# Local attention fed from an input transposed once per tile, with inverse norms formed as exp(-0.5 ln)

## What is computed

```
for i in range(DEPTH):                                   # DEPTH = 6
    x = attn_layer(shift_tokens(x), Wqkv[i], q_scale[i], k_scale[i], Wo[i]) + x
    x = ffn_layer(shift_tokens(x), ...) + x

def shift_tokens(t):                # upper half of the features comes from the token before
    a, s = jnp.split(t, 2, -1)
    s = jnp.pad(s, ((0, 0), (1, 0), (0, 0)))[:, :-1]
    return jnp.concatenate([a, s], -1)

def attn_layer(x, Wqkv, qs, ksc, Wo):                    # 16 heads of 64
    q, k, v = split heads of x @ Wqkv
    q = l2norm(q) * qs;  k = l2norm(k) * ksc             # t / max(|t|, 1e-12)
    q = q * cos * scale + rotate_half(q) * sin * scale   # k with 1 / scale
    # blocks of 32 queries see their own and the preceding 32 keys, within a band
    sim = q . k * 8, masked;  out = softmax(sim) . v
    return out @ Wo
```

## Time and profile before

| | us |
|---|---|
| span of the profiled execution | 8256.2 |
| unprofiled runs, median of 3 | 8264.78 |
| lowest, highest | 8245.68, 8279.47 |
| PE busy | 6903.7 (84%) |
| DVE busy | 5790.4 (70%) |
| ACT busy | 3976.8 (48%) |
| POOL busy | 2842.2 (34%) |

### The profile page before, as it was taken

How to read it: one execution, slowest core, us unless ns; L and a number is a source line. 1 busy time by engine, 2 the same in 40 slices (tenths; PEclk the granted TensorE clock), 3 DMA queues, 4 the chain that set the end, 5 groups by cost and what they waited for, 6 DMA issues and landing times. The chain is left out here.

```text
span 8256.2 us, 273787 instructions
## 1 busy us (share of the span) xinstructions
PE 6903.7 (84%) x119720; PEld 4913.8 (60%) x119720; DVE 5790.4 (70%) x10595; ACT 3976.8 (48%) x6628; POOL 2842.2 (34%) x2110
## 2 busy tenths in 40 slices
PE   7999699999996998998998998998997779445566
PEld 3444478888885665665665665665665556345434
DVE  6666389999996885885885885885886557752366
ACT  3555145555553774775775775775775212210121
POOL 0101033323332773773773773773772000001000
PEclk8999599999998999999999999999998889555556
DMA  0000000000001221221221221221220000000000
GB/s 15 1 1 1 3 6 4 4 4 4 4 3 33 69 69 45 69 69 41 71 72 41 69 72 42 69 69 45 69 72 24 2 15 1 3 3 4 5 0 13
DMA packets 187955, 249.19 MB, mean 30 GB/s; under 512 B 58997, under 2 KB 85492, under 8 KB 185844
## 3 DMA queue, kind: packets, MB, share of 16 engines
q1 hardware_dynamic: 186740, 231.40, 10.6%
HBM read 27.84 MB, written 2.10 MB: 4 GB/s over the span
## 5 line engine op out<-in xcount | busy, mean ns | idle before, releaser
L1701 POOL TENSOR_TENSOR XNT<-XNT 128x1024 f32<-128x1024 f32 x384 | 908.8, 2367 | 309.0 <-DVE XNT L1875 309.0
L1775 PE MATMUL wa_front<-w_wqkv,wa_xsT 128*128 128x512 f32 x1920 | 951.6, 619 | 49.9 <-ACT wa_kT L1756 29.6
L1704 POOL TENSOR_TENSOR XNT<-XNT,wa_rnorm 128x1024 f32<-128x1024 f32 x320 | 608.8, 1902 | 349.1 <-DVE wa_rnorm L1883 349.1
L1872 DVE TENSOR_TENSOR XNT<-wa_front,w_scaled 128x1024 f32<-128x1024 f32 x320 | 381.7, 1193 | 292.8 <-ACT wa_sq L1721 292.8
L1775 PEld LDWEIGHTS wa_front<-w_wqkv,wa_xsT 128*128 128x128 f32 x1920 | 333.4, 193 | 314.0 <-issue 281.8
L446 PE MATMUL a0h_ring<-a0h_QT,a0h_KT 32*128 32x512 f32 (+3 forms) x1536 | 448.7, 556 | 14.3 <-ACT a0h_E L564 10.4
L564 ACT ACTIVATE a0h_E<-a0h_ring 128x512 f32<-128x512 f32 (+1 forms) x640 | 320.6, 555 | 287.6 <-PE a0h_ring L446 285.8
L1721 ACT ACTIVATE wa_sq<-wa_front 128x1024 f32<-128x1024 f32 x320 | 324.9, 1015 | 185.5 <-PE wa_front L1775 184.9
L1875 DVE TENSOR_TENSOR XNT<-wa_front,w_scaled 128x512 f32<-128x512 f32 x640 | 408.6, 680 | 0.0
L1887 DVE TENSOR_REDUCE wa_norm<-wa_sq 128x16 f32<-128x1024 f32 x320 | 386.8, 1209 | 0.0
L1781 PEld LDWEIGHTS wa_front<-consts,XNT 128*128 128x128 f32 x2560 | 292.7, 143 | 141.8 <-POOL XNT L1704 66.8
(11 more groups left out here) (632 smaller groups left out, 18051.1 us busy)
## 6 DMA issues: line engine op xcount, KB each, us to landing
wa_v_look<-wa_v_all SPq DMA_DIRECT2D x960, 128.0 KB, 2.4
wa_v_look<-wa_v_all SPq DMA_DIRECT2D x640, 64.0 KB, 2.0
wal_v_look<-wal_v_all SPq DMA_DIRECT2D x192, 128.0 KB, 2.3
wal_v_look<-wal_v_all SPq DMA_DIRECT2D x128, 64.0 KB, 2.0
w_wqkv<-in_L_ffn_Wqkv_dram SPq DMA_DIRECT2D x6, 1024.0 KB, 6.0
w_wo<-in_L_ffn_Wo_dram SPq DMA_DIRECT2D x6, 512.0 KB, 6.7
w_wqkv<-in_L_ffn_Wqkv_dram SPq DMA_DIRECT2D x12, 256.0 KB, 7.1
f2w_raw<-in_L_ffn_w_dram SPq DMA_DIRECT2D x48, 64.0 KB, 1.9
```

The source lines that it names most:

```text
L1701: g.tensor_tensor(rot[:, at], rot[:, at], part[:, at], ALU.add).then_inc(s[summed], 1)
L1704: g.tensor_tensor(rot[:, at], rot[:, at], spread(rnorm[:, at, :], HDW), ALU.mult).then_inc(s[done], 1)
L1775: last = pe.matmul(front[:, first + i, :], xsT[:, slot, :], wqkv[:, (2 * n + i) * 512:(2 * n + i + 1) * 512], start=True, stop=True)
L1872: v.tensor_tensor(rot[:, n], src, cos, ALU.mult)
```

## The change

The shifted input is no longer made by three products. A new stage of the pipeline, `fetch`, runs one step ahead of `turn_in` (so there is a 36th step, k = -1). PE transposes the tile once, straight out of `Y`, into the first bank of the Q product's PSUM pair, and ACT copies the two halves to `xT`, the upper half one column further right. `xT` holds the eight tiles of a sequence side by side, for two sequences, and its column 0 is zero; `x_of` gives the 128 columns of a tile. `y`, `xsT` and the POOL copy are gone.

The DVE operation on `norm` is now a `tensor_scalar` with one tensor input instead of a `tensor_tensor` with two, and the DVE reciprocals of the norms are gone.

The order on the engines changes too. The K product is squared by ACT at the start of the next step instead of at the end of its own, and the rotation of K waits for the product, not for the square. DVE makes both sums of squares and both clamps before the rotation of Q. ACT does the two parts of the K norm ahead of the copy to `pT`.

```diff
         @block.gpsimd
-            if turn_in is not None:
-                before(g, "xsT_ps")
-                g.tensor_copy(y[:, u], Y[:, ds(turn_in + 1, 1), :]...).then_inc(s["y_copied"], 1)
...
-                    now(g, rnorm_in, 2)
+                    now(g, rnorm_in)
         @block.scalar
-            def root(n, ready, done):
+            def inverse_root(n, ready, used, logged, done):
                 now(a, ready)
-                a.activation(norm[:, n, :], norm[:, n, :], ACT.Sqrt).then_inc(s[done], 1)
+                a.activation(log[:, n, :], norm[:, n, :], ACT.Ln, scale=LOG_SCALE).then_inc(s[logged], 1)
+                now(a, logged)
+                before(a, used)
+                a.activation(rnorm[:, n, :], log[:, n, :], ACT.Exp, scale=-0.5, bias=unscale[:]).then_inc(s[done], 1)
...
             if project is not None:
-                a.activation(primed[:, 1:2], primed[:, 0:1], ACT.Sqrt)
-                root(K, "k_norm_in", "k_root")
+                before(a, "k_norm_in")
+                square(K, "k_part", "sq_k")
                 before(a, "q_norm_in")
                 square(Q, "q_ps", "sq_q")
+                inverse_root(K, "k_clamped", "k_rot", "k_log", "k_rnorm")
...
-            if turn_in is not None:
-                now(a, "xsT_ps")
-                before(a, "v_ps")
-                a.activation(xsT[:, u, :], back[:, 1, 0:P], ACT.Copy).then_inc(s["xsT_ready"], 1)
             if project is not None:
+                inverse_root(Q, "q_clamped", "q_rot", "q_log", "q_rnorm")
...
-                root(Q, "q_norm_in", "q_root")
-                a.activation(primed[:, 1:2], primed[:, 0:1], ACT.Exp)
...
-            if turn_in is not None:
-                if project is not None:
-                    now(a, "k_norm_in")
-                square(K, "k_ps", "sq_k")
+            if fetch is not None:
+                buf, at = fetch // BLOCKS % 2, fetch % BLOCKS * P
+                now(a, "xT_ps")
+                a.activation(xT[0:HALFW, buf, at:at + P], front[0:HALFW, bank[Q], 0:P], ACT.Copy)
+                a.activation(xT[HALFW:P, buf, at + 1:at + 1 + P], front[HALFW:P, bank[Q], 0:P],
+                             ACT.Copy).then_inc(s["xT_ready"], 1)
         @block.tensor
-            if turn_in is not None:
-                x = back[:, 1, 0:P]
-                now(pe, "y_copied")
-                if attend is not None:
-                    now(pe, "pT_ready")
-                pe.matmul(x[0:HALFW], y[:, u, 0:HALFW], c.ident, start=True, stop=True)
-                pe.matmul(x[HALFW:P], y[:, u, HALFW:P], shifts[:, 0, :], start=True, stop=False)
-                pe.matmul(x[HALFW:P, 0:1], y[:, w, HALFW:P], has_prev[:, 0, ds(turn_in % BLOCKS, 1)], ...)
             if project is not None:
-                before(pe, "sq_k")
+                now(pe, "sq_k")
                 now(pe, "k_part")
...
+            if fetch is not None:
+                if project is not None:
+                    now(pe, "q_part")
+                    now(pe, "sq_q")
+                else:
+                    before(pe, "xT_ready")
+                pe.transpose(front[:, bank[Q], 0:P], tile(Y, fetch + 1), c.ident).then_inc(s["xT_ps"], 1)
         @block.vector
-            def invert(n, root_in, done):
-                now(v, root_in)
-                v.tensor_tensor(norm[:, n, :], norm[:, n, :], least[:], ALU.max).then_inc(s[done], 1)
-                v.wait_ge(s[done], 2 * project + 1)
-                v.reciprocal(rnorm[:, n, :], norm[:, n, :]).then_inc(s[done], 1)
+            def clamp(n, norm_in, done):
+                now(v, norm_in)
+                v.tensor_scalar(norm[:, n, :], norm[:, n, :], 1e-24, None, ALU.max).then_inc(s[done], 1)
...
-                rotate(K, "sq_k", "kT_ps", "k_part")
+                rotate(K, "k_ps", "kT_ps", "k_part")
...
-                invert(K, "k_root", "k_rnorm")
+                square_sums(K, "sq_k", "k_norm_in", "k_log")
+                clamp(K, "k_norm_in", "k_clamped")
+                square_sums(Q, "sq_q", "q_norm_in", "q_log")
+                clamp(Q, "q_norm_in", "q_clamped")
                 rotate(Q, "sq_q", "qT_ps", "q_part")
-                square_sums(Q, "q_norm_in", "q_rnorm")
...
-                invert(Q, "q_root", "q_rnorm")
```

More of the change, by code:

```diff
@@ L11 @@
+import math
 from contextlib import ExitStack
@@ L1483 @@
 QK_SCALE = 8.0
+LOG_SCALE = 2.0 ** 16
 UNITS = int(P * 4 * 2 / 3)
@@ L1590, in l1_ffn_stage, with window_attention_steps @@
             st.end_step()
-def window_attention_steps(nc, st, Y, XNT, c, scaled, band, has_prev, shifts, wqkv, wo, loads):
+def window_attention_steps(nc, st, Y, XNT, c, scaled, band, has_prev, wqkv, wo, loads):
     H, A, W = HEADSW, HEADSW // 2, P // WINDOW
@@ L1635, in by_parity @@
         return x.rearrange("p (a k) x -> p k a x", k=2)
-    TURN, PROJECT, SCORE, ATTEND = range(4)
+    FETCH, TURN, PROJECT, SCORE, ATTEND = range(-1, 4)
     begins = {}
-    for stage, names in ((TURN, "y_copied xsT_ps xsT_ready k_ps sq_k"),
-                         (PROJECT, "q_ps v_ps v_ready v_moved sq_q k_norm_in q_norm_in k_root q_root k_rnorm q_rnorm q_part k_part "
+    for stage, names in ((FETCH, "xT_ps xT_ready"),
+                         (TURN, "k_ps"),
+                         (PROJECT, "sq_k q_ps v_ps v_ready v_moved sq_q k_norm_in q_norm_in k_clamped q_clamped k_log q_log k_rnorm q_rnorm q_part k_part "
                                    "q_sum q_rot k_sum k_rot qT_ps kT_ps qT_ready kT_ready"),
@@ L1772, in _, with product @@
         def _(pe):
-            def product(n, first, done, slot):
+            def product(n, first, done, which):
                 for i in range(2):
-                    last = pe.matmul(front[:, first + i, :], xsT[:, slot, :], wqkv[:, (2 * n + i) * 512:(2 * n + i + 1) * 512],
+                    last = pe.matmul(front[:, first + i, :], x_of(which), wqkv[:, (2 * n + i) * 512:(2 * n + i + 1) * 512],
                                      start=True, stop=True)
@@ L1785, in _ @@
             if project is not None:
+                if project == 0:
+                    before(pe, "xT_ready")
                 before(pe, "qT_ready")
-                product(Q, bank[Q], "q_ps", w)
+                product(Q, bank[Q], "q_ps", project)
             if attend is not None:
@@ L1807, in _ @@
                 last.then_inc(s["scores_ps"], 1)
-            if turn_in is not None:
-                x = back[:, 1, 0:P]
-                now(pe, "y_copied")
-                if attend is not None:
-                    now(pe, "pT_ready")
-                pe.matmul(x[0:HALFW], y[:, u, 0:HALFW], c.ident, start=True, stop=True)
-                pe.matmul(x[HALFW:P], y[:, u, HALFW:P], shifts[:, 0, :], start=True, stop=False)
-                pe.matmul(x[HALFW:P, 0:1], y[:, w, HALFW:P], has_prev[:, 0, ds(turn_in % BLOCKS, 1)], start=False,
-                          stop=True).then_inc(s["xsT_ps"], 1)
             if project is not None:
-                before(pe, "sq_k")
+                now(pe, "sq_k")
                 now(pe, "k_part")
-                product(2, bank[K], "v_ps", w)
+                product(2, bank[K], "v_ps", project)
             if attend is not None:
                 now(pe, "pT_ready")
-                if turn_in is not None:
-                    now(pe, "xsT_ready")
                 pe.wait_ge(s["v_moved"], 16 * MOVES * (attend + 1))
@@ L1845, in _ @@
                 last.then_inc(s["oT_ps"], 1)
+            if fetch is not None:
[3 more added lines that the diff above has]
+                else:
+                    before(pe, "xT_ready")
+                pe.transpose(front[:, bank[Q], 0:P], tile(Y, fetch + 1), c.ident).then_inc(s["xT_ps"], 1)
             if turn_in is not None:
-                now(pe, "xsT_ready")
+                before(pe, "xT_ready")
                 if project is not None:
                     now(pe, "kT_ready")
-                product(K, bank[K], "k_ps", u)
+                product(K, bank[K], "k_ps", turn_in)
             if project is not None:
@@ L1853, in _ @@
                 now(pe, "sq_q")
+                if fetch is not None:
+                    now(pe, "xT_ready")
                 turn(Q, bank[Q], "qT_ps")
@@ L1940, in _ @@
         def _(g):
-            for buffer in (y[:, 1], kT[:, 0, :, 0:WINDOW], v_all[:, 1]):
+            for buffer in (xT[:, :, 0:1], kT[:, 0, :, 0:WINDOW], v_all[:, 1]):
                 last = g.memset(buffer, 0.0).then_inc(s["zeroed"], 1)
@@ L1953, in _ @@
         def _(a):
+            a.preload_act_table_set("natural_log_exp_and_others")
             a.wait_ge(s["pads_zeroed"], 1)
+            a.wait_ge(s["zeroed"], 3)
         @block.tensor
@@ L1961, in tile_of @@
             return k - stage if 0 <= k - stage < TILES else None
-        for k in range(TILES + 3):
-            pipeline_step(block, k, turn_in=tile_of(k, TURN), project=tile_of(k, PROJECT), score=tile_of(k, SCORE),
+        for k in range(-1, TILES + 3):
```

(1 more changed line is left out.)

29 lines of the change are left out of this document (12 added, 17 removed).

## The result

The changed kernel took 8287.39 us in the median of 20 runs (8264.58 to 8302.71), the kernel before, on the same chip, 8268.69 (8244.22 to 8279.76). The ratio is 1.0024, with a 95% interval of 1.0016 to 1.0032: some 19 us slower. The forecast was 8256 us, 9 us faster; the time lies in the range of 8120 to 8325 and within the 0.5% of "same". The profiled executions spanned 8280.6 us after and 8256.2 before.

The account below looks back on a forecast made before the run. PE was taken to bound the kernel before, the ring the changed one: +13 us for 192 tiles, +6 edges, -28 hidden stalls, together -9 from 8265 to 8256 us, range 8120 to 8325.

Parts of the forecast that it names:

- PE part: Local attention on PE: 0.45 us wait and 0.43 us of products go, 0.13 us transpose comes; step 15.22 to 14.47 us.
- Waits at `o`: PE's wait at the turning of `o`, until DVE has made it: 0.30 us a step, to stay.
- held clamp: DVE's second clamp (Q) in a step, blocked by POOL's product of K until its end, some 1.3 us long.
- rival of the free clamp: Q's clamp on DVE is not held by POOL; PE bounds at 14.47 us a step, total 8130 us; chance 0.20.
- 8.53 and 7.40: When DVE's clamp of Q ends, held or free, in us from the end of POOL's last product with `rnorm` (Q).
- 1.15: Microseconds taken off the ring if DVE's clamp of Q is not held: 15.29 - 1.15 = 14.14 us.
- reciprocal of the row sum held too: Rival: POOL's addition for K holds DVE's row-sum reciprocal; +0.6 us in the ring, total 8370 us; chance 0.04.
- the ring: Dependency loop over PE, ACT, DVE and POOL between successive Q products with `rnorm` on POOL: 15.29 us, bounding the step.
- POOL's wait for itself: Term of the ring: POOL's wait between its addition and its product for Q, 0.06 us.
- price of the pointer: About 93 ns more for ACT's exp with a bias pointer; ring 15.38 us and total 17 us more, given as estimate.
- hidden stalls: PE issue stalls at the product with V, 0.75 of each 0.9 us absorbed by slack: -28 us (0 to -35).
- edges: The 36th step of each of six layers, about 1 us of latency each: +6 us (0 to 12).

Follow-up runs that it names:

- e1: The changed kernel with a DVE reciprocal in place of each clamp and exp's scale sign changed, lower bound left out; 8124.87 us, ratio 0.9817 to the kernel before.
- e2: The changed kernel without the two clamps, 1e-24 entering as a bias in ACT's logarithm instead; 8105.63 us, ratio 0.9804 to the kernel before.
- e7: The kernel before with only ln and exp for inverse norms, old order, three products kept, clamps replaced by a bias in the logarithm; 8316.86 us, ratio 1.0061.
- e3: The changed kernel with DVE's rotation of Q moved ahead of the second sum of squares and clamp; 8613.94 us in one run.
- e4: The changed kernel with scale 1 in the logarithm and no bias tensor in exp; 8272.1 us, ratio 0.9993 to the kernel before.

## Why the prediction came out as it did

- **The PE part held.** 14.47 us was forecast for a step that only PE bounds; e1 and e2 measured 14.43 and 14.42. Waits at `o` stayed (7.4 us in 25 waits in e1, 7.3 in 24 before).
- **The held clamp held.** It was to end with POOL's product, some 1.3 us long; it took up to 1.44 and ended 0.03 after it, and the first clamp took 0.17. The rival of the free clamp was priced at 8130 us; e1 gave 8124.87 and e2 8105.63. (By the prediction's own 8.53 and 7.40 its 1.15 should be 1.13; nothing hangs on it.) The step of these two was as priced, but that the totals come so near is partly luck: in e1's trace the untouched parts take 44 us more than in the two of the kernel before, and its first steps and its stalled steps 15 and 21 less. The rival "reciprocal of the row sum held too" did not come: reciprocals took 0.25 us beside POOL everywhere.
- **The waits came where they were forecast:** about 0.7 us ahead of the turning of `o` (0.80 in the step shown, 0.65 in the mean of 25) and 0.3 ahead of Q (0.43, and 0.45 in the mean of 22).
- **The first step that failed is the ring's sum,** 15.29 us against 15.39, in two of its terms. Exp was put at the 0.22 of the root and takes 0.31, and POOL's wait for itself was put at 0.06, from two memsets, and is 0.15 between addition and product (3405.42 + 2.36 to 3407.93). The two make 0.18; the other pieces came out 0.08 shorter together (the sum of K's squares until its clamp 1.20 instead of 1.24, the clamp's end to POOL's addition 2.40 instead of 2.43). I had set the price of the pointer aside as a sentence beside the sum. The Trainium skill (ScalarE: Activation LUTs, section "What ACT_TABLE_LOAD costs") has about 93 ns for a bias pointer; the trace agrees, with 92. Its estimate, 15.38 us and 17 us more in all, was the better one, in part by luck, since it has neither POOL's 0.15 nor the pieces that were shorter. In the median step the miss is 0.10 us, or 19 us in the total; the measured growth of the step is 0.17, 31 us in 186 steps.
- **The hidden stalls:** 28 us forecast and 38 measured, since the excess over 186 median steps fell from 47 to 9 us. The reason holds for less than half of it. The prediction let PE stall as before and later slack absorb the stalls. But PE stalls for 46 us in these steps of the kernel before, in both traces, and for only 22 and 24 in those of the changed kernel. So some 23 us are stalls that did not come, which nothing in the prediction forecast and whose cause is open, and some 14 were absorbed.
- **The edges:** +6 us forecast, +10 measured, as -3.6 at the first steps and +13.8 at the last. In these last steps the traces have 10.7 and 11.8 us of issue stalls on PE before, 19.3 and 19.9 after, 7 of them at the scores, where there were none. They too go with PE's instructions: e7 has 11.6 and none at the scores, the seven other variants 18.8 to 20.7. That accounts for some 8 of the 14 us.
- **The second step that failed is one that stood in no sentence:** that what isn't touched stays the same. Outside local attention the means differ by 19 us, which is most of the 22 by which the spans differ; within it the change cost 3 us, against -9 forecast. So the ring moved the sum by about +18 above the forecast, the stalls by -10, the edges by +4, and the untouched code by +19: from -9 to +22.

What stays open: why PE's issue stalls in unchanged code come more often once the attention's own PE instructions are others. It goes with them (28 times in three traces, 34 or 35 in nine). It is not the whole of it: e1 differs from the changed kernel in three lines, none of them on PE, and its untouched parts, 2661.0, 455.4 and 1993.1 us, are 26 us longer together than the changed kernel's in the first of its traces. That the place of the code in memory matters is a guess that no run here tests. The 7 us ahead of local attention are within what two executions of the changed kernel differ by (12), so they may be chance; over all twelve traces this part takes 2629.3 to 2661.0 us, with the same code in each.

## What to carry to other kernels

Before a small DVE operation on SBUF is put ahead of something that others wait for, look up what POOL does at that time; here 0.17 us became 1.44 and ate a gain of some 160 us, and a reciprocal in the same place, or an added term in ACT's bias, gave it back. Follow the ring over all engines once when a bound engine is relieved, with every small handover priced from its own kind of row, since an error of 0.1 us there counts 192 times. And do not read a difference of 20 us in 8260 as the edit's own before the untouched parts of the two traces have been set side by side.

## What the runs showed of the hardware

- The exclusion between DVE and POOL depends on the operation, not on size: at 128x16 a `tensor_scalar` within SBUF was held for up to 1.27 us beyond its 0.17, a reciprocal of the same tile not at all (in e1, 192 of them lie wholly inside a POOL operation, and none takes over 0.255). The sum of squares over 128x1024, from SBUF to SBUF, ran in 1.21 us while POOL was busy all the time (e3, at 3400.50), and 174 of them lie wholly inside a POOL operation in the kernel before, at 1.21 us each. The Trainium skill's rule in SBUF — State Buffer, section "SBUF: two separate sides", that the loser blocks for the whole of the other's instruction, is stated there only for DVE instructions in a two-port mode or with two inputs from SBUF. The trace agrees: the old clamp has two such inputs, the new one is a `tensor_scalar`, and the reciprocal and the sum, with one input each, ran free.
- Slack hides stalls of an engine, as two kernels with equal stalls on PE show: in e4, which the ring bounds, 28.0 us of issue stalls lengthen the 186 steps by 9 us, in e1, which PE bounds, 27.1 us lengthen them by 26.
- A wait of PE can cost granted clock as well: in e3 it idled for 2.26 us and then ran at the lower level, 0.51 granted, for some 3 us; such steps are 1.1 us longer than the others.
- Dropping work from engines with slack can make a kernel slower: in e7 ACT is busy for 3577 us instead of 3977 and DVE for 5687 instead of 5790, and each step is 0.34 us longer, because what remained stands ahead of one copy that PE waits for.
